# Two adjacency units per edge window, both issued behind the window's eight products

## What is computed

```
edge_index = stack([src, dst])
x = layernorm(x + L0(x, edge_attr_128, src, dst))   # agg = segment_sum(edge_attr, dst); relu([agg, x] @ W1 + b1) @ W2 + b2
x = layernorm(x + L1(x, edge_index))                # agg = segment_sum(x[src], dst), dense, two batch norms
x = layernorm(x + L2(x, edge_index))                # twice: mean over neighbours, dense
x = layernorm(x + L3(x, edge_index, edge_attr_16))  # attention over edges (3 heads), dense, layer norm
```

## Time and profile before

| | |
|---|---|
| median of three runs | 3326.29 us (3325.86 to 3333.78) |
| profiled execution | 3322.32 us |
| its span | 3320.7 us |
| TensorE matmul busy | 2399.7 us (72%), 21724 instructions |
| TensorE weight load busy | 2076.2 us (63%) |
| VectorE busy | 1563.3 us (47%) |
| GpSimd busy | 1430.9 us (43%) |
| ScalarE busy | 704.2 us (21%) |
| mean granted TensorE clock | 0.816 |

### The profile page before, as it was taken

One profiled execution on the slowest core, in us unless ns is written; L12 is line 12 of the kernel. 1 busy time (PEld: TensorE's weight loads), 2 busy tenths in 40 slices (PEclk: granted clock), 3 DMA queues, 4 the chain that ended last, 5 costly groups with the idle time before them and its releaser, 6 DMA issues. The chain is left out here.

```text
span 3320.7 us, 68789 instructions
## 1 busy us (share of the span) xinstructions
PE 2399.7 (72%) x21724; PEld 2076.2 (63%) x21725; DVE 1563.3 (47%) x3763; ACT 704.2 (21%) x1093; POOL 1430.9 (43%) x1498
## 2 busy tenths in 40 slices
PE   1599999989899962999969992666530103999965
PEld 0466666679688841888859882566530103999954
DVE  5476666623311165111133335888879201555567
ACT  0077777726200042000010000000000100000033
POOL 4322222213200012122224446777778777776765
PEclk9899999989899975999989996777775555555577
DMA  4378888942688815888869995999972534655611
GB/s 129 99 226 275 275 279 283 285 146 70 182 284 282 282 46 170 252 248 250 249 196 296 290 292 137 184 186 189 182 170 76 160 106 117 153 142 145 144 37 43
DMA packets 560771, 627.36 MB, mean 189 GB/s; under 512 B 265887, under 2 KB 412524, under 8 KB 560041
## 3 DMA queue, kind: packets, MB, share of 16 engines
q1 hardware_dynamic: 258425, 387.60, 38.1%
q10 hardware_dynamic: 252072, 164.25, 19.6%
q0 software_dynamic: 50208, 74.70, 9.3%
HBM read 484.61 MB, written 142.11 MB: 189 GB/s over the span
## 5 line engine op out<-in xcount | busy, mean ns | idle before, releaser
L896 POOL DMA_INDIRECT rows<-x_rows,src_i x832 | 854.1, 1027 | 279.5 <-issue 236.1
L1570 PE MATMUL ps<-slices,wide 128*128 128x250 f16 x7350 | 829.0, 271 | 41.9 <-DMA slices<-adjacency 36.0
L1570 PEld LDWEIGHTS ps<-slices,wide 128*128 128x128 f16 x7350 | 715.9, 98 | 130.6 <-issue 24.2
L1802 PE MATMUL ps<-slices 128*128 128x75 bf16 x4992 | 248.2, 227 | 160.4 <-DVE slices L2544 160.4
L1802 PEld LDWEIGHTS ps<-slices 128*128 128x128 bf16 x4992 | 241.7, 118 | 166.9 <-issue 166.9
L936 POOL TENSOR_TENSOR ea_one<-ea,ones 128x64 f32<-128x64 f32 x250 | 133.9, 536 | 464.0 <-DMA ea<-in_edge_attr 447.0
L1510 PE MATMUL ps<-weighted,slices 128*128 128x57 f32 x1120 | 253.1, 417 | 69.5 <-DVE weighted L2124 69.5
L1510 PEld LDWEIGHTS ps<-weighted,slices 128*128 128x128 f32 x1120 | 247.1, 333 | 69.8 <-DVE weighted L2124 69.8
L1456 PE MATMUL ps<-rows,weighted 128*32 128x128 f32 x2000 | 274.5, 282 | 15.4 <-DMA ea<-in_edge_attr 13.4
L1510 PE MATMUL ps<-weighted,rows 128*128 128x57 f32 x544 | 130.6, 418 | 194.2 <-DMA rows<-x_rows,src_i 170.8
L1510 PEld LDWEIGHTS ps<-weighted,rows 128*128 128x128 f32 x544 | 123.4, 332 | 197.1 <-issue 171.0
(11 more groups left out here) (356 smaller groups left out, 3421.4 us busy)
## 6 DMA issues: line engine op xcount, KB each, us to landing
slices<-adjacency SPq DMA_DIRECT2D x525, 437.5 KB, 5.5
rows<-in_edge_attr SPq DMA_DIRECT2D x250, 256.0 KB
adjacency<-wide ACTq DMA_DIRECT2D x91, 437.5 KB, 3.1
adjacency<-slices ACTq DMA_DIRECT2D x84, 437.5 KB, 3.1
x_of_edges<-rows SPq DMA_DIRECT2D x140, 256.0 KB
slices<-x_of_edges ACTq DMA_DIRECT2D x140, 256.0 KB
slices<-src_low ACTq DMA_DIRECT2D x52, 512.0 KB
rows<-x_rows,src_i POOLq DMA_INDIRECT x832
```

Source lines behind the costliest of these rows:

```text
L896: pool.indirect_dma_start(out=packed[i][:, c, :], out_offset=None, in_=table, in_offset=bass.IndirectOffsetOnAxis(ap=rows_of, axis=0)).the ...
L1570: mm = pe.matmul(ps_d[b], high_low[:, part, QS * s + q, :], slices[:, s, PN * q:PN * (q + 1)], start=(s == 0 and q == 0 and part == 0), st ...
L1802: mm = pe.matmul(ps_g[:, s, b, c, 0:HEADS * QH], lowT[:, s, b, h, P * c:P * (c + 1)], tab_b[:, n, h, :, :].rearrange("p h i -> p (h i)"), ...
```

## The change

In `window` the two calls of `unit` stand behind the feature products. Before, unit n stood ahead of the window's waits and its row products, and unit n+1 between row products and feature products.

```diff
             def window(w, v, i, pair, s, t=None, n=0):
 
-                if t is not None and n < NU:
-                    unit(t, n)
                 pe.wait_ge(onehot_ready, pair + 1)
                 pe.wait_ge(*arrived0(i, v))
                 to = ps_w[s][LO * i:LO * (i + 1), :]
                 for c in range(CH):
                     pe.matmul(to[:, 0:P], onehot_l[i // 2][:, c, i % 2, :], packed[i][:, c, :], start=(c == 0), stop=(c == CH - 1))
-                if t is not None and n + 1 < NU:
-                    unit(t, n + 1)
                 pe.wait_ge(ea_ready, w + 1)
                 for c in range(CH):
                     mm = pe.matmul(to[:, P:P + NSUM], onehot_l[i // 2][:, c, i % 2, :], ea_one[:, i, c, :],
                                    start=(c == 0), stop=(c == CH - 1))
                 mm.then_inc(group_summed, 1)
+                if t is not None and n < NU:
+                    unit(t, n)
+                if t is not None and n + 1 < NU:
+                    unit(t, n + 1)
```

## The result

The changed kernel took 3307.56 us (median of six runs, 3300.54 to 3313.56), the kernel before 3326.07 us on the same chip (six runs, 3321.72 to 3333.78). The ratio is 0.9945, with an interval of 0.9927 to 0.9962: 18.5 us faster. The profiled execution took 3307.64 us, 14.7 less than that of before.

The account below looks back on a forecast made before the run. The prediction took a loop through the last store's landing to bound the blocks. Terms: -1.3 - 22 x 0.18 (-4.0) + 2.9 = -2.4 us on 3322.3, so 3319.9; the median stands 4.0 above, giving 3324 us, range 3308 to 3339.

Parts of the forecast that it names:

- What bounds the stage: Blocks, 169 to 660 us: a loop of copies ending with the last store's landing sets the pace, 19.60 us a block.
- TensorE alone: Windows with two units take 2.23 us instead of 2.45; seven such windows save 1.5 us of TensorE per block.
- First copy to fourteenth: ScalarE's copies within a block, walked one by one: 15.05 us instead of 15.49, 0.44 us less.
- the tail: End of a block's copies: the fourteenth starts 0.6 us behind the thirteenth, at 15.05 us, where ScalarE before idled 0.59 us.
- Is the first unit still in time?: Block head: the next block's first unit is ready 2.9 us after the fourteenth copy, ahead of the landing at 4.1 us.
- The cover: Block head: 1.2 us between the next first unit being ready and the landing; if gone, 1.23 us paid per block.
- Fourteenth copy to landing: Block end: last store issued 0.44 us sooner, but the DMA queue holds its landing; the block gains only 0.18 us.
- The clock: TensorE at block heads: four falls from 2.4 to 1.2 GHz instead of two, 1.46 us each, +2.9 us.
- My sign for this part: TensorE's clock: more than two stretches near 0.57 would prove the forecast wrong.
- First two blocks: Start of the stage, no landing to wait for: -1.3 us for the two together, between 0 and -2.8.
- the landing sooner in full: Rival, block end: the landing gains all 0.44 us in 22 blocks, -15 us, 3311 us; chance 0.16.
- my two signs: Block end: fourteenth copy to next first copy staying at 4.1 us, or a block under 19.2 us.

Follow-up runs that it names:

- half loads: Row loads behind the first four windows bring half their bytes: changed kernel 3283.20 us, kernel before 3296.14 us, one execution each.
- early stores: Seven stores behind copies 0, 1, 3, 5, 7, 9 and 11: changed kernel 3284.93 us, ratio 0.9875; kernel before 3302.35 us, ratio 0.9892; other versions too.
- the read ahead of the wait: Changed kernel with SyncE's register read of a window's address moved ahead of its wait for the buffer: 3317.25 us, ratio 0.9980.
- one store moved alone: Kernel before, with a block's last store issued ahead of the fourteenth copy's wait instead of behind that copy: 3322.15 us, ratio 0.9981.
- three more reads: Kernel before, with SyncE making three more register reads ahead of each load: 3471.40 us, ratio 1.0441.
- one more register read: Kernel before, with SyncE making one more register read ahead of each load: 3362.02 us, ratio 1.0060.
- one unit on each side: Against the changed kernel, one unit ahead of a window's eight products and one behind, the products kept together: 3338.80 us, ratio 1.0026.
- both units ahead: Against the changed kernel, both units moved ahead of the window's waits and its eight products: 3312.81 us in one execution.
- the late report: Changed kernel, with a window's buffer handed back by the first product of its second unit instead of its last feature product: 3307.37 us, ratio 0.9950.

## Why the prediction was wrong

**What bounds the stage** was right: a loop through the last store's landing. The experiments with half loads in the new order and with early stores show it, since both let the block fall to where TensorE releases the first copy.

**TensorE alone.** Forecast 2.23 us per window, measured 2.23. The rule of the Trainium skill that a change of tiling mode drains the engine (TensorEngine Tiling (Array Packing), Key Properties) agrees with that in its sign: two changes of the shape fewer per window, 0.22 us less. That this saving would not be passed on was right, too: the order with the same saving was slower than before.

**First copy to fourteenth.** Forecast 15.05, measured 15.12, and the walk holds on the way (C3, C5, C7 and C9 at 3.36, 5.98, 8.57 and 11.12; measured 3.38, 6.06, 8.50 and 11.21). Units 2 and 3 start 1.36 and 2.49 us behind C0 as worked out. One detail of the tail was off. I had ScalarE finish C12 and start C13 0.6 us later without idling, and so it does (0.58 us in the rows), but I did not see that C13 was then queued and the issue behind it would leave first. The last issue came 14.89 us behind C0 instead of 15.19.

**Is the first unit still in time?** Forecast 2.9 us behind C13, measured 3.01 wherever no store stood in the way. The cover held in all blocks: the store was last in each block but the first two.

**Fourteenth copy to landing** is the step that failed. I wrote that the last store "is now issued 0.44 us sooner, but the store before it is not (C11 stays at 13.4), and the loads come as before", and from that took 4.37 us. Both halves were wrong. The issues of the seven stores before stood 0.32, 3.68, 6.13, 9.03, 11.29, 13.57 and 15.62 us behind C0, and stand now at 0.32, 3.28, 5.55, 8.20, 10.66, 13.11 and 14.89: every one but the first is 0.4 to 0.8 sooner. It is not the copies that moved by so much: C5, C9 and C11 are within 0.06 us of where they stood (C3 is 0.16 sooner, C7 0.49, C13 0.36). C11 did stay, at 13.48 before and 13.46 now; what moved is the store behind it. Before, it left once C11 had started (C11 of that block started at 421.67):

```profile
421.76 0.34 ACTq L1096 DMA_DIRECT2D adjacency<-slices  x1
```

which is 13.58 us behind 408.18. Now it leaves 0.34 us ahead of C11 (431.55 and 431.89 in the rows above), because each odd unit follows its even one at once, so that the odd copy stands queued behind the even one and the issue passes it. That is the detail of the tail again, in five more places, and the forecast had it in none. And the loads do not stay where they were, counted from C0: windows end sooner ahead of the last store, but SyncE takes 0.7 us more to send each load, so that two loads still leave 0.8 and 2.7 us behind it. With that delay taken back (the read ahead of the wait) one of them leaves 0.54 us ahead of the last store, at the median, and the block is 19.40 us, within 0.02 of my sum, though by other terms: the seven stores leave as in the change, and still only 0.20 of the 0.88 us are left. No run has the change's stores with loads just as prompt as before, so how the 0.88 us divide between the stores' move and the loads' stays open. Measured was 3.55 us at the median and 3.78 as a mean, so 22 blocks gave 6.8 us here, where I had 22 x 0.26 = 5.7 us of loss. My argument, that the queue holds the last store, is true of one store moved alone (0.1 us gained of 1.23) and was applied to a change that moved six of seven and the loads besides. Put by the issue, I had the last store leave 0.43 us sooner and take 0.27 longer to land; it left 0.73 sooner and took 0.17 less.

**The clock.** Forecast four falls, measured three. The first of them, TensorE around it:

```profile
283.37 0.62 PE L1445 MATMUL ps<-aT,prod 128*128 128x245 f16 x4 [1.31 <-ACT wide L1109]
284.49 0.69 PE L1445 MATMUL ps<-aT,prod 128*128 128x245 f16 x4 [0.51 <-ACT wide L1109]
285.12 1.91 PE L1454 MATMUL ps<-rows,weighted 128*32 128x128 f32 x8
```

The eight row products take 1.91 us instead of 1.06: the granted clock is 1.2 instead of 2.4 GHz for 3.4 us, from 284.9 on. It is the head of a block whose first copy waited long for a store:

```profile
282.03 3.54 ACT L1109 ACTIVATE wide<-ps 128x980 f16<-128x980 f32 x3 [3.48 <-DMA adjacency<-wide]
```

Window 1's products were done in that wait, so the hole ahead of unit 2 is 1.31 us instead of 0.20. C0 to C13 was 16.58, 16.33 and 16.47 in the three blocks, so 1.2 to 1.5 us each, as the forecast's 1.46. Over the runs (one profiled execution each, the one with three more reads left aside), the number of falls inside the blocks went roughly with how long the first copies waited: ten with one more register read, five with one unit on each side, four with the read ahead, one or two in three others, and none with both units ahead, with the late report, with half the loads, or in any version with early stores. My sign for this part contradicted the forecast: more than two falls were to prove me wrong, and I had forecast four.

**First two blocks.** Forecast -1.3, measured -2.8, at the end of the bound that I gave.

**The sum.** Measured: -2.8 for the first two blocks, -7.2 for C0 to C13 of the other 23 (23 x -0.36 and 1.1 for one more fall of the clock), -6.8 for the 22 landings: -16.8 of the 16.9 us. Forecast: -1.3, -9.7, +5.7 and +2.9. The landing accounts for 12.5 us of the 14.4 between the two sums. The rival that came nearest is the first, the landing sooner in full (3311 us), to which I gave 0.16; its time was right within 4 us. One of my two signs for it came (a block under 19.2 us). Its reason, loads asked for at more even distances, is in the trace: the longest distance between two loads of a block fell from 3.8 to 2.8 us at the median. But no run tests it by itself, and it does not order the runs: both units ahead has 3.9 us and a block of 19.23, one unit on each side 3.1 and 19.87, the read ahead 3.9 and 19.40, the late report 2.8 and 18.88. I had the last store's issue in that rival only 0.44 us sooner, so nearness of its time is in part luck.

**What stays open.** Which timing of the loads is good for a store's landing follows no simple rule here: prompt loads cost 0.7 us a block in the new order, late ones cost 0.3 us of landing in the old, and with ten falls of the clock 0.6 of a block. The count of bytes describes it after the fact; it would not have foretold it.

## What to carry to other kernels

When a wait ends with the last transfer of a queue that is full, ask of the change which of all transfers in that queue it moves and by how much, those of other engines included, before taking the landing as fixed. Here one reordering of compute gained 0.9 us a block and another lost 0.3 through that landing; moving the urgent transfers forward is the direct remedy (36 us of the kernel's time in the old order and 39 in the new, against 18 for the change), and after it the order no longer mattered. Where an issue stands behind a compute instruction in an engine's program, ask too whether that instruction is queued or has to wait: here this moved stores by 0.5 to 0.6 us whose copies had not moved.

## What was not expected of the hardware

- A register read by SyncE from on-chip memory takes 0.27 us at the median before and 0.97 us after. Why is open. The stores alone do not explain it: with the late report all stores leave at the same places as in the change and the read takes 0.28 us, and within the change some 18 packets of stores were under way in the first 0.27 us of a slow read (0.8 us or more) and 14 in those of a fast one (under 0.5). Taking this delay away cost 0.7 us a block, so that it helped here was chance.
- Four such reads per load made SyncE the bound of the stage, at 3 us a window (ratio 1.0441).
- ScalarE issues a DMA that stands behind a queued copy before this copy starts, 0.23 us ahead of it (414.71 and 414.94). Whether a copy is queued or waits for its input shifts the issue by 0.36 us.
